# Scan of a delta-rule layer: the state's decay product moved from VectorE to GpSimd

## The chip, the cores and the metric

The kernel runs on one core of a Trainium2 chip. The metric is the device time of one execution in microseconds (us), the median over several runs. Engines are called TensorE (PE in profile rows, PEld for its weight loads), VectorE (DVE), ScalarE (ACT), GpSimd (POOL) and SyncE (SP); each works through its own instruction list in order, and they meet only at semaphores.

## The reference

A block of three parts on x of 4 x 1024 tokens, 256 wide: a mixture-of-experts feed-forward layer, an attention-like recurrent layer, and the feed-forward layer again. Only the recurrent layer is touched. Its core, cut to what matters (8 heads of 32, so 4 x 8 = 32 states of 32 x 32):

```
k = l2norm(silu(x @ Wk));  k_ = -beta * k
gk = interleave(log_f, 0);  a = interleave(k_ * exp(log_f), k_);  b = interleave(k, k)
kk, vv, qq = interleave(0, k), interleave(0, v), interleave(0, q)
def step(S, inp):
    g, a_t, b_t, k_t, v_t, q_t = inp
    bS = einsum('bhk,bhkv->bhv', b_t, S)
    S = exp(g)[..., None] * S + a_t[..., None] * bS[:, :, None, :] + k_t[..., None] * v_t[:, :, None, :]
    o = einsum('bhk,bhkv->bhv', q_t, S)
    return (S, o)
```

## The kernel before

The 1024 tokens of a batch row are done in 4 passes of 256 tokens. In each pass a preparing part forms the projections, the decays and the inverses of small triangular matrices, and then a scan carries the states through the pass. The scan has UN = 16 steps of CT = 16 tokens. A step takes a state S of the 32 chains (128 partitions x 256 numbers, in two halves f = 0, 1 of 128 x 128) to the next one. The four passes come one after the other, each scan starts and ends as a block of its own, and the feed-forward layers lie outside.

In step u, for each half f, the work is:

1. TensorE, line 2387 ("r"): the state against the step's decayed keys and queries, `kq`, after the state S[f] of step u-1 is there.
2. VectorE, line 2461 ("Rt"): adds the values `vi`; line 2464 ("R"): transposes in 32 x 32 blocks.
3. VectorE, line 2466 ("D"): D[f] = S[f] times the decay of the whole step, `eg`. It stands behind the transpose R of its half, so ahead of Rt of the second half.
4. After both halves VectorE does line 2452 ("turn"): the transpose of the end keys `kd` **of step u+1**, behind a wait on `s_kd` for step u+1. In steps 6 to 13 of a pass that has another pass behind it, it then does line 2470, the statistics of one row block for the next pass.
5. TensorE, line 2395 ("u"), ScalarE, line 2432 ("U": the copy out of PSUM), TensorE, line 2404 ("d"), in that order for each half; TensorE does u of both halves ahead of d of both. A filler product (line 2409) closes the step.
6. VectorE, line 2475 ("dS"): transposes the state's increment out of PSUM; line 2478 ("S add"): S[f] = D[f] + dS[f], and releases `s_S[f]`. The order is dS 0, S add 0, dS 1, S add 1.

GpSimd forms the operands of a step in `stage` (lines 2345 to 2360): two products at line 2355 and one at 2356 (`kq`), a copy at 2357 (`vi`) and two products at 2359 (`kd`, whose second releases `s_kd`). There are two buffers of each. The stages of steps 0 and 1 are made before the scan opens. In the scan, stage(u+1) waits for r and Rt of step u-1, and for the turn of step u-1, because it writes over their buffer; nothing else stands ahead of it in GpSimd's list. ScalarE makes copies of other operands (2424, 2425) and of the outputs (2435) beside this.

The semaphore `s_S[f]` has value 1 at the start and is raised once in each step, so "s_S[f] at least u+1" means that step u-1 has stored its state. `s_dec[f]` says that D[f] of a step is done.

Of the kernel before, what the change touches and what calls it, by code (L numbers as in the profile page):

```python
# [10 lines left out]
ALU = mybir.AluOpType  # L11
ACT = mybir.ActivationFunctionType
AX = mybir.AxisListType
P = 128
# [27 lines left out]
HEADS, HD = 8, 32  # L42
# [4 lines left out]
CT = 16  # L47
SUB = 2 * CT
UN = 16
PT = CT * UN  # L50
PASSES = SEQ // PT
GS = CT + 1
# [1857 lines left out]
def invert_and_scan(nc, scope, sb, sem, psum, s, nxt, env, z, a_sb, a_top, tk, s_tk, tm):  # L1910
# [8 lines left out]
    zz, pr = tb("zz", [P, HQ * CT * CT]), tb("pr", [P, 3, HQ * CT * CT])  # L1919
    pr_all = pr[:, :, :].rearrange("p n x -> p (n x)")  # L1920
    steps = scan(sem, psum, s, env, z, nxt, a_sb[:, :, :].rearrange("p g c -> p (g c)")[:, SUB * HQ * SUB:], ng, pr_all, zz)

    s_zero, s_one, s_tp, s_ev, s_fine = sem("zero"), sem("one"), sem("tp"), sem("gev"), sem("fine")
# [373 lines left out]
def scan(sem, psum, s, env, z, nxt, home0, home1, home2, home3):  # L2297


    k, q, kb, v, eg, ek, ta, S, ident = (env[n] for n in "k q kb v eg ek ta S ident".split())  # L2300
    o, xa, stats, s_pre, s_nxt = env["o"], env["xa"], env["stats"], z["pre"], z["nxt"]
    NT = BATCH * PT // P
    HC = CHAINS // 2
# [3 lines left out]
    def carve(home, shapes):  # L2307
# [11 lines left out]
    Rt, R, D, U = halves[0:2], halves[2:4], halves[4:6], halves[6:8]  # L2319
# [9 lines left out]
    s_r, s_u, s_d, s_Rt, s_R, s_dec, s_dS, s_S, s_U, s_O = ([sem(f"{n}{f}") for f in range(2)] for n in  # L2329
        ("r", "u", "d", "Rts", "Rs", "dec", "dSs", "Ss", "Us", "Os"))  # L2330
# [14 lines left out]
    def stage(pool, u, b, first):  # L2345
        def t(x, at=0, step=CT):
            return x[:, :, bass.ds(u * step + at, CT)]
        if not first:
            pool.wait_ge(s_r[1], u - 1)
            pool.wait_ge(s_kr, u - 1)  # L2350
            pool.wait_ge(s_Rt[1], u - 1)
        keys = kq[b][:, :, 0:SUB].rearrange("p c (t r) -> p c t r", r=2)
        ends = kd[b].rearrange("p c (t r) -> p c t r", r=2)
        for r in range(2):
            pool.tensor_tensor(keys[:, :, :, r], t(kb), t(eg, r, GS), ALU.mult)
        pool.tensor_tensor(kq[b][:, :, SUB:KQ], t(q), t(eg, 1, GS), ALU.mult).then_inc(s_kq, 1)
        pool.tensor_copy(vi[b][:, :, :, 1], t(v)).then_inc(s_vi, 1)
        for r in range(2):
            i = pool.tensor_tensor(ends[:, :, :, r], t(k), t(ek, r, GS), ALU.mult)
        i.then_inc(s_kd, 1)  # L2360

    def open_gpsimd(pool, u):
        pool.memset(vi[u][:, :, :, 0:1], 0.0).then_inc(s_pad, 1)
        stage(pool, u, u, True)

    def gpsimd(pool):
        with pool.Fori(1, UN // 2) as j:
            for b in range(2):
                stage(pool, 2 * j + b, b, False)

    def tensor(pe):
        def step(u, b):
# [75 lines left out]
    def vector(dve):  # L2448
        def turn(u, b):
            dve.wait_ge(s_kd, u + 1)  # L2450

            dve.transpose(ar[b][:, :, CT:KQ], kd[b][:, :, :]).then_inc(s_kr, 1)

        def step(u, b, last, row=None):
            for f in range(2):
                ch = slice(HC * f, HC * f + HC)
                if f == 0:
                    dve.wait_ge(s_vi, u + 1)
                dve.wait_ge(s_r[f], u + 1)

                dve.tensor_tensor(Rt[f][:, :, :], vi[b][:, ch, :, :].rearrange("p c t r -> p c (t r)"),
                                  b_p[f][:, :, 0:SUB], ALU.add).then_inc(s_Rt[f], 1)
                dve.wait_ge(s_Rt[f], u + 1)
                dve.transpose(R[f][:, :, :], Rt[f][:, :, :]).then_inc(s_R[f], 1)  # L2464
                dve.wait_ge(s_S[f], u + 1)
                dve.tensor_tensor(D[f][:, :, :], S[:, ch, :], eg[:, ch, bass.ds(u * GS + CT, 1)].to_broadcast([P, HC, HD]), ALU.mult).then_inc(s_dec[f], 1)
            if not last:
                turn(u + 1, 1 - b)
            if row is not None:
                dve.bn_stats(stats[:, bass.ds(row, 1), :].rearrange("p a s -> p (a s)"),  # L2470
                             xa[:, bass.ds(row, 1), :].rearrange("p a d -> p (a d)")).then_inc(s_stat, 1)
            for f in range(2):
                ch = slice(HC * f, HC * f + HC)
                dve.wait_ge(s_d[f], u + 1)
                dve.transpose(dS[f][:, :, :], b_p[f][:, :, KQ:RO]).then_inc(s_dS[f], 1)
                dve.wait_ge(s_dec[f], u + 1)
                dve.wait_ge(s_dS[f], u + 1)
                dve.tensor_tensor(S[:, ch, :], D[f][:, :, :], dS[f][:, :, :], ALU.add).then_inc(s_S[f], 1)
        for f in range(2):
            dve.sem_inc(s_S[f], 1)  # L2480
        dve.wait_ge(s_pad, 2)
        turn(0, 0)
        step(0, 0, False)
        step(1, 1, False)
        with dve.Fori(1, STAT // 2) as j:
            for b in range(2):
                step(2 * j + b, b, False)
        if nxt is not None:
            dve.wait_ge(s_nxt, 16 * BATCH)
        with dve.Fori(STAT // 2, (STAT + NT) // 2) as j:  # L2490
            for b in range(2):
                step(2 * j + b, b, False, 2 * j + b - STAT if nxt is not None else None)
        step(UN - 2, 0, False)
        step(UN - 1, 1, True)
        if nxt is not None:
            dve.wait_ge(s_stat, NT)

    return Scan(sync, open_gpsimd, gpsimd, tensor, open_scalar, scalar, vector)


# [58 lines left out]
```

## Time and profile before

| | |
|---|---|
| median of 3 runs | 1867.22 us (1866.78 to 1869.74) |
| the profiled execution's own time | 1866.42 us |
| its span in the profile | 1864.6 us |
| busy in the span: PE, DVE, ACT, POOL | 1593.2, 1126.5, 774.5, 760.1 us |
| the four scans | 64 steps; the first runs from 641.2 to 708.5 us |
| mean granted TensorE clock | 0.932 of full |

The span is what the profile records; some 2 us lie around it. Timeline rows have the start, the duration, the engine, the line, the operation, the tile written and read, how many instructions are merged in the row, and in brackets how long the engine had been idle and which engine's work ended that.

### The profile page before, as it was taken

How to read it: one execution, taken by the hardware profiler on the slowest of the kernel's cores; microseconds unless marked ns; L12 is line 12 of the kernel's file. 1: busy time of each engine (PE TensorE's matmuls, PEld its weight loads, DVE VectorE, ACT ScalarE, POOL GpSimd, SP SyncE). 2: the span in 40 equal slices, each digit the busy share in tenths (PEclk: the TensorE clock that was granted, in tenths of full speed). 3: DMA queues.
4: the chain of work that ended last, by engine and by line, in shares of the span. 5: the costliest groups of instructions: out<-in, count | busy, mean ns of one | idle time of the engine just before them, and what ended most of it. 6: DMA issues, size and time to landing. Idle time of an engine off the chain costs nothing. (4 is left out here: it accounts for less than half of the span.)

```text
span 1864.6 us, 69187 instructions
## 1 busy us (share of the span) xinstructions
PE 1593.2 (85%) x26524; PEld 1302.6 (70%) x26525; DVE 1126.5 (60%) x3424; ACT 774.5 (42%) x1805; POOL 760.1 (41%) x944
## 2 busy tenths in 40 slices
PE   5499999999577988788888788887885999999994
PEld 5499999999435565355654556545564999999994
DVE  7646434444357786877868778688774546444341
ACT  2143333333267334673346733467332443333331
POOL 2554422222154651646516465164651234422221
PEclk9999999999779898798987999889897999999997
DMA  9563433232300200002000020000102833332334
GB/s 300 184 187 76 88 48 48 45 51 45 74 4 7 70 22 24 4 7 70 22 23 4 7 70 23 23 4 7 47 23 83 255 78 76 75 64 47 49 48 113
DMA packets 84233, 116.23 MB, mean 62 GB/s; under 512 B 12952, under 2 KB 74464, under 8 KB 82016
## 3 DMA queue, kind: packets, MB, share of 16 engines
q1 hardware_dynamic: 56160, 74.17, 13.1%
q0 software_dynamic: 27360, 37.80, 11.5%
q10 hardware_dynamic: 608, 2.96, 0.5%
q8 instruction: 54, 0.88, 0.2%
q14 instruction: 51, 0.42, 0.1%
HBM read 64.87 MB, written 54.21 MB: 64 GB/s over the span
## 5 line engine op out<-in xcount | busy, mean ns | idle before, releaser
L1065 POOL DMA_INDIRECT x<-ffn_yout,ffn_place x142 | 222.6, 1568 | 531.6 <-DVE ffn_yout L997 454.6
L1003 DVE TENSOR_TENSOR ffn_inner<-ffn_inner,ffn_bank 128x512 f32<-128x512 f32 x142 | 97.6, 687 | 349.2 <-PE ffn_bank L873 346.8
L873 PE MATMUL ffn_bank<-ffn_tileT,ffn_gate_now 128*128 128x128 f32 x2272 | 280.2, 277 | 0.0
L873 PE MATMUL ffn_bank<-ffn_tileT,ffn_up_now 128*128 128x128 f32 x2272 | 277.6, 275 | 0.0
L954 ACT ACTIVATE ffn_inner<-ffn_bank 128x512 f32<-128x512 f32 x142 | 84.8, 597 | 459.0 <-PE ffn_bank L873 459.0
L883 PE MATMUL ffn_bank<-ffn_w,ffn_inner 128*128 x1136 | 268.9, 380 | 1.7 <-DVE ffn_yout L997 1.7
L873 PEld LDWEIGHTS ffn_bank<-ffn_tileT,ffn_gate_now 128*128 128x128 f32 x2272 | 268.4, 194 | 0.1
L873 PEld LDWEIGHTS ffn_bank<-ffn_tileT,ffn_up_now 128*128 128x128 f32 x2272 | 266.1, 193 | 0.0
L883 PEld LDWEIGHTS ffn_bank<-ffn_w,ffn_inner 128*128 128x128 f32 x1136 | 205.0, 190 | 24.4 <-issue 2.5
L816 ACT COPY ffn_gate_now<-ffn_w 128x1024 f32 x142 | 148.4, 1045 | 29.9 <-issue 22.3
L816 DVE COPY ffn_up_now<-ffn_w 128x1024 f32 x142 | 99.6, 702 | 55.3 <-issue 43.9
L428 POOL DMA_INDIRECT xs<-at_kept_rows,at_kept_slots x64 | 78.8, 1231 | 115.7 <-ACT pass_aq L2218 73.7
L428 POOL DMA_INDIRECT xs<-ffn_rows,ffn_slot_u x80 | 80.1, 1001 | 51.6 <-DVE ffn_slot_u L335 27.8
L1860 PEld LDWEIGHTS at_bank<-at_ta 32*32 32x32 f32 x4096 | 61.1, 125 | 43.2 <-issue 43.0
L1860 PE MATMUL at_bank<-at_ta 32*32 32x48 f32 x4096 | 66.1, 227 | 13.6 <-DVE at_ta L1733 10.7
L997 DVE TENSOR_SCALAR ffn_yout<-ffn_bank,ffn_weight 128x256 f32<-128x256 f32 x142 | 67.4, 474 | 0.0
L2395 PE MATMUL at_wide<-pass_ng,pass_pr 32*32 32x32 f32 x3072 | 44.4, 196 | 26.1 <-DVE pass_ng L2464 12.6
L1870 PE MATMUL at_bank<-at_tm,at_consts 128*32 128x384 f32 x256 | 36.2, 644 | 29.8 <-POOL at_tm L1777 21.8
L2395 PEld LDWEIGHTS at_wide<-pass_ng,pass_pr 32*32 32x32 f32 x3072 | 36.5, 109 | 35.3 <-issue 35.3
L2404 PE MATMUL at_bank<-pass_pr,pass_ng 32*32 32x48 f32 x3072 | 54.7, 208 | 7.3 <-issue 2.3
L2228 ACT COPY at_ta<-at_bank 128x512 f32<-128x512 f32 x48 | 26.2, 593 | 80.3 <-PE at_bank L2124 79.1
L2432 ACT COPY pass_ng<-at_wide 128x128 f32<-128x128 f32 x96 | 25.5, 265 | 78.6 <-PE at_wide L2395 78.5
(574 smaller groups left out, 3179.3 us busy)
## 6 DMA issues: line engine op xcount, KB each, us to landing
ffn_w<-in_w1t_dram SPq DMA_DIRECT2D x16, 1024.0 KB, 5.6
ffn_tile<-xs SPq DMA_DIRECT2D x122, 130.0 KB, 2.1
ffn_w<-in_w2t_dram SPq DMA_DIRECT2D x16, 512.0 KB, 6.9
at_a_sb<-x SPq DMA_DIRECT2D x32, 256.0 KB, 2.8
ffn_x<-in_x_dram SPq DMA_DIRECT2D x16, 256.0 KB, 5.5
x<-ffn_x SPq DMA_DIRECT2D x16, 256.0 KB, 6.1
x<-at_a_sb SPq DMA_DIRECT2D x16, 256.0 KB, 2.1
xs<-ffn_empty SPq DMA_DIRECT2D x23, 130.0 KB, 2.9
```

The source lines that it names most:

```text
L428: pool.indirect_dma_start(xs, bass.IndirectOffsetOnAxis(ap=slot_u[:, c, i:i + 1], axis=0), rows[:, i, :], None).then_inc(s_scat, 16)
L816: copy(half_now[half][b][:, :, :], src.rearrange("p e k f -> p (e k) f")).then_inc(s_now[half], 1)
L873: t = pe.matmul(bank[:, i * P:(i + 1) * P], half_now[half][b][:, k, i * P:(i + 1) * P], rowsT[b][:, k * P:(k + 1) * P], start=(k == 0), st ...
L883: t = pe.matmul(p_y, inner[b][:, k * P:(k + 1) * P], w2[:, bass.ds(e * 1024 + k * DIM, DIM)], start=(k == 0), stop=(k == ICH - 1))
L954: act.activation(inner[b][:, :], p_g[b][:, :], ACT.Silu).then_inc(s_silu, 1)
L997: dve.tensor_scalar(yout[b][:, :], p_y, weight[b][:, 0:1], None, ALU.mult).then_inc(s_ys, 1)
L1003: dve.tensor_tensor(inner[b][:, :], inner[b][:, :], p_u[b][:, :], ALU.mult).then_inc(s_act, 1)
L1065: pool.indirect_dma_start(total, bass.IndirectOffsetOnAxis(ap=place[b][:, 0:1], axis=0), yout[b][:, :], None, compute_op=ALU.add).then_inc ...
L1860: t = pe.matmul(bank[r, uu * 2 * RW:(uu + 1) * 2 * RW], lo[r, u0 + uu, :, :].rearrange("p l c -> p (l c)"), hi[r, u0 + uu, :, :].rearrange ...
L1870: t = pe.matmul(p_f[x * HD:(x + 1) * HD, 0:UN // 4 * FE], headcol[:, :], prod[b][:, x * UN // 4 * FE:(x + 1) * UN // 4 * FE], start=True, ...
L2395: tiles(lambda c, r: pe.matmul(b_u[f][r, c * HD:(c + 1) * HD], tu[b][r, ch + c, :], R[f][r, c, :], start=True, stop=True)).then_inc(s_u[f], 1)
L2404: tiles(lambda c, r: pe.matmul(b_p[f][r, c, SUB:RO], U[f][r, c, :], ar[b][r, ch + c, :], start=False, stop=(c == HC - 1), skip_group_check ...
```

## The change

The product D is taken out of VectorE's list and put into GpSimd's. There D of step u stands ahead of the stage of step u+1, each half behind a wait for the state that step u-1 stores. It keeps its operands, its output and the semaphore that it raises.

```
     def open_gpsimd(pool, u):
         pool.memset(vi[u][:, :, :, 0:1], 0.0).then_inc(s_pad, 1)
         stage(pool, u, u, True)
 
+    def decayed(pool, u):
+        for f in range(2):
+            ch = slice(HC * f, HC * f + HC)
+            pool.wait_ge(s_S[f], u + 1)
+            pool.tensor_tensor(D[f][:, :, :], S[:, ch, :], eg[:, ch, bass.ds(u * GS + CT, 1)].to_broadcast([P, HC, HD]), ALU.mult).then_inc(s_dec[f], 1)
+
     def gpsimd(pool):
+        decayed(pool, 0)
         with pool.Fori(1, UN // 2) as j:
             for b in range(2):
+                decayed(pool, 2 * j + b - 1)
                 stage(pool, 2 * j + b, b, False)
+        decayed(pool, UN - 1)
```

and in VectorE's step, behind the transpose R of each half:

```
                 dve.transpose(R[f][:, :, :], Rt[f][:, :, :]).then_inc(s_R[f], 1)
-                dve.wait_ge(s_S[f], u + 1)
-                dve.tensor_tensor(D[f][:, :, :], S[:, ch, :], eg[:, ch, bass.ds(u * GS + CT, 1)].to_broadcast([P, HC, HD]), ALU.mult).then_inc(s_dec[f], 1)
```

## Rows read from the trace of the kernel before

**Rows 1.** One step of the first pass, step 10, on VectorE: the timeline
```profile
684.81 0.31 DVE L2464 STREAM_TRANSPOSE pass_ng<-pass_ng 128x128 f32<-128x128 f32 x1
685.05 0.25 DVE L2466 TENSOR_TENSOR pass_ng<-at_S,at_eg 128x128 f32<-128x128 f32 x1
...
685.22 0.28 DVE L2461 TENSOR_TENSOR pass_ng<-at_a_sb,at_bank 128x128 f32<-128x128 f32 x1
...
685.93 0.43 DVE L2452 STREAM_TRANSPOSE pass_pr<-pass_ng 128x256 f32<-128x256 f32 x1
...
686.29 0.38 DVE L2470 BATCH_NORM_STATS2 at_stats<-at_a_sb  x1
...
686.85 0.32 DVE L2475 STREAM_TRANSPOSE pass_zz<-at_bank 128x128 f32<-128x128 f32 x1 [0.17 <-PE at_bank L2404]
...
687.27 0.61 DVE L2478 TENSOR_TENSOR at_S<-pass_ng,pass_zz 128x128 f32<-128x128 f32 x1
```

**Rows 2.** Timeline: GpSimd's stage(11), and step 9's S add of half 1
```profile
681.22 0.28 DVE L2461 TENSOR_TENSOR pass_ng<-pass_ng,at_bank 128x128 f32<-128x128 f32 x1
...
681.85 0.90 POOL L2355 TENSOR_TENSOR pass_ng<-at_qb,at_eg 128x128 f32 x2 [1.59 <-DVE pass_ng L2461]
...
683.36 0.94 POOL L2359 TENSOR_TENSOR pass_ng<-at_kfk,at_ek 128x128 f32 x2
...
683.52 0.32 DVE L2475 STREAM_TRANSPOSE pass_zz<-at_bank 128x128 f32<-128x128 f32 x1
...
683.94 0.51 DVE L2478 TENSOR_TENSOR at_S<-pass_ng,pass_zz 128x128 f32<-128x128 f32 x1
```

**Rows 3.** Timeline: TensorE's r of half 1 in step 10; the last step's end and what follows
```profile
684.59 0.54 PE L2387 MATMUL at_bank<-at_a_sb,at_S 32*32 32x48 f32 x32 [0.24 <-DVE at_S L2478]
...
707.54 0.29 DVE L2478 TENSOR_TENSOR at_S<-pass_ng,pass_zz 128x128 f32<-128x128 f32 x1
...
708.21 0.29 DVE L2478 TENSOR_TENSOR at_S<-pass_ng,pass_zz 128x128 f32<-128x128 f32 x1
709.57 1.28 ACT L1424 ACT_TABLE_LOAD   x1 [1.22 <-PEq L70]
```

**Rows 4.** Timeline: the Rt add that opens steps 2, 6 and 14
```profile
651.90 0.29 DVE L2461 TENSOR_TENSOR pass_ng<-at_a_sb,at_bank 128x128 f32<-128x128 f32 x1 [0.89 <-PE at_bank L2387]
...
668.21 0.29 DVE L2461 TENSOR_TENSOR pass_ng<-at_a_sb,at_bank 128x128 f32<-128x128 f32 x1
...
700.76 0.29 DVE L2461 TENSOR_TENSOR pass_ng<-at_a_sb,at_bank 128x128 f32<-128x128 f32 x1
```

**Rows 5.** One line's instructions: durations in ns, minimum/median/maximum, of D and one stage product
```profile
L2466 DVE TENSOR_TENSOR pass_ng<-at_S,at_eg x96: 247/249/251, 641.8 to 1172.4; 128x128 f32<-128x128 f32 x96
...
L2356 POOL TENSOR_TENSOR pass_ng<-at_qb,at_eg x24: 411/433/456, 638.1 to 1165.3; 128x128 f32 x21, 128x128 f32<-128x128 f32 x3
```

**Rows 6.** Timeline: a wait of GpSimd outside the loop, and its shortest stage
```profile
636.82 0.28 DVE L2071 TENSOR_TENSOR pass_a_top<-pass_a_top,pass_pr 128x128 f32<-128x128 f32 x1
...
637.15 0.21 POOL L2363 MEMSET pass_ng<- 128x128 f32 x1 [1.94 <-DVE pass_a_top L2071]
...
690.01 0.82 POOL L2355 TENSOR_TENSOR pass_ng<-at_qb,at_eg 128x128 f32 x2 [1.86 <-DVE pass_ng L2461]
...
691.40 0.83 POOL L2359 TENSOR_TENSOR pass_ng<-at_kfk,at_ek 128x128 f32 x2
```

**Rows 7.** Timeline: step 1, where TensorE is late
```profile
645.38 0.29 DVE L2478 TENSOR_TENSOR at_S<-pass_ng,pass_zz 128x128 f32<-128x128 f32 x1
...
649.66 0.32 DVE L2475 STREAM_TRANSPOSE pass_zz<-at_bank 128x128 f32<-128x128 f32 x1 [1.96 <-PE at_bank L2404]
```

**Rows 8.** Stretches: busy us (count) of PE, PEld, DVE, ACT, POOL; granted clock; DMA share; GB/s
```profile
644.00:648.00 4.00, 2.11 (x105) 1.56 (x91) 3.22 (x11) 0.93 (x4) 1.71 (x5) 1.00 0.45 152
648.00:652.00 4.00, 3.77 (x179) 3.35 (x183) 1.24 (x5) 1.46 (x6) 1.56 (x5) 0.65 0.02 4
656.00:704.00 48.00, 38.90 (x2296) 31.88 (x2296) 40.19 (x139) 17.30 (x71) 26.13 (x66) 1.00 0.07 22
```

## The prediction

> **What bounds the kernel now.** I read the busy table first: TensorE 85% of the span, GpSimd 41%. That is an average over stages, and it says nothing about a scan, so I went to the timeline of one step. Inside a scan TensorE is busy 38.90 us of 48 and GpSimd 26.13 us of 48 [rows 8]: both have gaps, and a step is a chain through several engines. It takes 4.08 us where VectorE has no statistics (16.31 us for the four steps from 651.90 to 668.21) and 4.07 us where it mostly has (32.55 us for the eight to 700.76) [rows 4]. The statistics cost next to nothing, because VectorE still waits 0.17 us for TensorE's d behind them [rows 1]. The scan's last S add ends at 708.50 and the next block opens behind it [rows 3], so what the 64 steps gain or lose goes whole into the time.
>
> Two things in the step matter here. First, the slot of D: the transpose R starts at 684.81, D at 685.05, Rt of the second half at 685.22 [rows 1]. Second, GpSimd's slack. Stage(11) runs from 681.85 to 684.30 [rows 2], and VectorE's turn, which waits for its last product, comes at 685.93 [rows 1]: it is 1.63 us early. It is early only because it may start 0.35 us behind Rt of step 9 (681.50), while step 9 still has its second half to go [rows 2].
>
> **What is removed.** Two D of 249 ns on VectorE in each step [rows 5]. D of half 0 holds Rt of half 1 back by at most its slot, 0.17 us. But Rt of half 1 also needs TensorE's r of half 1, which began at 684.59, 0.63 us before it [rows 3]. The r's own last product ends at 685.13, so at most 0.1 of the 0.17 us is free in a step like this; D of half 1 stands ahead of the turn, in time that VectorE spends waiting. I take 0.15 us for a step that isn't held otherwise, and nothing where GpSimd holds it.
>
> **What is moved, and past what.** D(u) now stands ahead of stage(u+1) in GpSimd's list, and its second half waits for S add 1 of step u-1. The stage behind it has no need of that state, but it queues behind the wait. The turn of step u waits for that stage, and in VectorE's list dS and both S adds of step u stand behind the turn. So a new ring closes: S add 1 of step u-1, D, the stage, turn, dS, S add, dS, S add 1 of step u. Its length, from the end of one S add 1 to the end of the next:
>
> - GpSimd wakes: the nearest rows are 0.35 us in the loop, with three waits and computed addresses [rows 2], and 0.05 us outside it (637.10 to 637.15) [rows 6]. D has one wait and an address to compute: 0.25 us.
> - D on GpSimd: same size as a product of the stage, 433 ns (411 to 456) [rows 5]: 0.43. That is 1.7 times VectorE's 249 ns.
> - The stage: 2.45 us (681.85 to 684.30) [rows 2], or 2.22 (690.01 to 692.23) [rows 6]: 2.35.
> - VectorE wakes for the turn: no row has VectorE waiting for GpSimd. TensorE began 0.14 us after the S add that freed it (684.45 to 684.59) [rows 2, 3], the shortest wait of GpSimd was 0.05, the longest 0.35: I take 0.10.
> - Turn to the next instruction: 0.36 us (685.93 to 686.29). With statistics 0.38 more, no longer hidden [rows 1].
> - dS 0 to S add 0: 0.42 (686.85 to 687.27) [rows 1].
> - S add 0's start to S add 1's end: 0.96 undisturbed (707.54 to 708.50) [rows 3]. Here GpSimd's D 0 of the next step begins some 0.54 us in (0.29 and the 0.25 of the wake) and ends at 0.97; S add 1 would begin at 0.67. An S add under a GpSimd product ends 0.15 us behind it (684.30 and 684.45) [rows 2]. So 0.97 and 0.15, some 1.14, of which 0.18 is contention.
>
> The sum is 0.25+0.43+2.35+0.10+0.36+0.42+1.14 = 5.05 us, and 5.43 with statistics: 0.97 and 1.36 us more than now. TensorE's path doesn't come close. In step 10 dS 0 followed the end of step 9's S add 1 by 2.40 us (684.45 to 686.85) [rows 1, 2], and in the ring it follows by 3.49.
>
> **How many steps.** Step 0 has its stage beforehand, and step 15 has no stage behind its D: both keep the old chain and gain 0.15. Step 1 is already late by TensorE: its dS 0 begins 3.99 us after the S add 1 before it ended (645.67 to 649.66) [rows 7], later than the ring's 3.49, so only the 0.18 is added. That leaves 13 steps: in the first three passes 8 with and 5 without statistics, 8 x 1.36 + 5 x 0.97 + 0.18 - 0.30 = 15.6 us; in the last 13 x 0.97 + 0.18 - 0.30 = 12.5 us. In all 3 x 15.6 + 12.5 = 59.3 us. On the profiled execution's own 1866.4 that gives 1925.7; the median of the runs is 0.8 above it, so 1927.
>
> **The port.** An S add, with two inputs in SBUF, was stretched from 0.29 to 0.51 and 0.61 us, while a dS transpose out of PSUM kept its 0.32 under a running stage product [rows 1 to 3]. No row has an Rt add (one input in SBUF, one in PSUM) under a GpSimd product; in the changed kernel all of them are. If they took turns, each would hold the stage back by up to its 0.28 us, 0.56 a step, and the ring would be 5.6 us.
> The Trainium skill, SBUF — State Buffer, Who interferes with whom, says that a VectorE instruction with at most one SBUF input doesn't contend with GpSimd. By that rule the Rt adds cost nothing and the sum stays; without it 52 steps pay up to 0.56 us each, 29 us.
>
> **Rivals.**
> 1. *The Rt adds (or GpSimd's added waits) lengthen the ring*, by about half of the 0.56: 0.3 us in 52 steps is 16 us, 1943. For it: the S adds show that the two engines do block each other. Against: the dS row. 12%.
> 2. *TensorE's clock.* After a stretch in which TensorE was busy 2.11 of 4 us, the granted clock of the next was 0.65 [rows 8]. In the ring it would be busy some 3.3 of 5.1 to 5.4 us, so it may fall to 1.2 GHz. In the ring this is mostly hidden: with every product chain longer by half, d's result comes at about 3.6 instead of 2.4 us after S add 1, against the turn's end at 3.5. Steps 0, 1 and 15 would pay about 0.9 us each: 4 x 3 x 0.9 = 11 us, 1938. 13%.
> The Trainium skill, TensorE: Matmul & The Clock Gate, What's actually happening, has it that the slow level is the default and activity releases it; that speaks for this rival, as does the 0.65.
> 3. *Faster: GpSimd takes D in its idle time*, and only VectorE's slot is left to count: up to 64 x 0.17 = 11 us, less what r of half 1 takes back, so 1860. For it: GpSimd idles 1.59 us ahead of a stage [rows 2]. It decides by one place: stage(11) must end before the turn's old slot, 685.93, thus 1.48 us after the S add at 684.45, where wake, D, stage and wake need 3.13. Against it stands the order of the list: the idle time lies ahead of the old stage, and the new wait uses all of it. 3%.
> 4. *Only contention*: the ring has cover that I don't see and the S adds alone are stretched: 0.18 x 56 is 10 us, less 64 x 0.05 to 0.10: about 1872. 2%.
>
> **How the numbers follow.** The ring as summed has 69%; 1% is left for no change. The unknown costs at their low ends (wake 0.05, D 0.41, stage 2.22, turn's wake 0.05, no contention) take 0.58 us off 52 steps, 30 us; at their high ends (0.36, 0.46, 2.46, 0.35, the full 0.61 of an S add) they add 0.64, 33 us. They will hardly all fall on one side: two thirds of that is 1907 and 1949, and the upper side takes in rivals 1 and 2, so 1907 to 1952. About 0.2% is what a measurement of this kernel can tell from no change. Faster by over 0.2%: 0.03; within: 0.01; slower: 0.96.
>
> **What would show it.** The Rt adds that open steps 2 to 14 stand 5.0 to 5.5 us apart, wider by 0.3 to 0.4 where there are statistics. VectorE's longest idle time in a step lies ahead of line 2452 (the turn), released by GpSimd's second `kd` product. GpSimd's D 1 begins 0.05 to 0.36 us behind S add 1 and its stage runs on without a gap. S add 1 takes 0.4 to 0.6 us, S add 0 takes 0.29. The idle time ahead of dS, put down to TensorE, is gone. Steps 0 and 15 keep some 4 us. If the turn doesn't wait and steps stay near 4.0, the ring is wrong and rival 3 holds; if the Rt adds or the stage's products are longer than before, it is rival 1; if the granted clock within the scans is well under 1, rival 2.

## The result, and the profile after

The changed kernel takes 1904.83 us (median of 4 runs, 1903.83 to 1906.46) against 1868.48 us for the kernel before beside it: a ratio of 1.0196, 95% interval 1.0179 to 1.0212. It is slower by 36 us. Forecast were 59 us, with a range from 1907 to 1952, so the direction held and the size didn't: the time lies 2 us under the range.

A step of the scan in the timeline (step 10 of the first pass, from the S add that ends step 9; VectorE's and GpSimd's rows, where [rows 1, 2] have those of before):

```profile
679.07 0.44 DVE L2485 TENSOR_TENSOR at_S<-pass_ng,pass_zz 128x128 f32<-128x128 f32 x1
...
679.60 0.29 DVE L2470 TENSOR_TENSOR pass_ng<-pass_ng,at_bank 128x128 f32<-128x128 f32 x1
...
679.70 0.41 POOL L2370 TENSOR_TENSOR pass_ng<-at_S,at_eg 128x128 f32<-128x128 f32 x1 [0.33 <-DVE at_S L2485]
...
680.06 0.83 POOL L2355 TENSOR_TENSOR at_a_sb<-at_qb,at_eg 128x128 f32 x2
680.26 0.29 DVE L2470 TENSOR_TENSOR pass_ng<-pass_ng,at_bank 128x128 f32<-128x128 f32 x1
...
681.46 0.83 POOL L2359 TENSOR_TENSOR at_a_sb<-at_kfk,at_ek 128x128 f32 x2
...
682.32 0.45 DVE L2461 STREAM_TRANSPOSE pass_pr<-at_a_sb 128x256 f32<-128x256 f32 x1 [1.43 <-POOL at_a_sb L2359]
...
682.69 0.38 DVE L2477 BATCH_NORM_STATS2 at_stats<-at_a_sb  x1
683.00 0.29 DVE L2482 STREAM_TRANSPOSE pass_zz<-at_bank 128x128 f32<-128x128 f32 x1
...
683.39 0.29 DVE L2485 TENSOR_TENSOR at_S<-pass_ng,pass_zz 128x128 f32<-128x128 f32 x1
...
683.87 0.41 POOL L2370 TENSOR_TENSOR pass_ng<-at_S,at_eg 128x128 f32<-128x128 f32 x1 [1.58 <-DVE at_S L2485]
...
684.02 0.40 DVE L2485 TENSOR_TENSOR at_S<-pass_ng,pass_zz 128x128 f32<-128x128 f32 x1
```

Lines have moved: D is L2370, Rt L2470, the turn L2461, dS L2482, the S add L2485. The ring can be read off row by row. S add 1 ends at 679.51, GpSimd's D 1 starts at 679.70, the stage at 680.06 and without a gap to 682.29; VectorE has stood idle for 1.43 us and starts the turn at 682.32; then come the statistics, dS, S add 0, dS, S add 1, which ends at 684.42. dS has no idle time in front of it: TensorE's result has long been there. In [rows 1] the turn had none and dS had 0.17 us.

The instructions of the turn's line in the whole run (first their durations in ns, then what the idle time ahead of them waited for, in us and times):

```profile
L2461 DVE STREAM_TRANSPOSE pass_pr<-at_a_sb x24: 402/445/447, 644.1 to 1199.0; 128x256 f32<-128x256 f32 x24
...
  POOL at_a_sb L2359: 35.7, 26
  POOL pass_ng L2359: 28.2, 21
  POOL end_ng L2359: 9.6, 7
```

54 turns waited for GpSimd's `kd` product, 73.5 us in all; there were none before. The scans grew by less than half of that (below), since much of it stands in the place of other idle time: VectorE idled 34.6 us ahead of dS before and 16.5 after.

The steps, taken from the timelines of both kernels as the distance from one S add 1's end to the next, in us, first pass, steps 1 to 15:

```
before  5.34 4.90 4.09 4.13 4.04 4.05 4.09 4.10 4.04 4.05 4.08 4.10 4.04 3.78 4.00
after   5.42 4.75 4.59 4.55 4.68 5.07 4.91 4.88 4.99 5.08 4.90 4.88 4.97 4.61 4.04
```

Over all passes, with steps 3 to 14 as the body of a scan: the 24 with statistics went from a mean of 4.08 to 4.96, the 24 without from 4.03 to 4.63. That is 24 x 0.887 + 24 x 0.596 = 35.6 us. Steps 0, 1, 2 and 15 gave back 2.4 us in all. The four scans took 275.7 us before (from the first Rt add to the last S add) and 308.9 after: 33.2 us more. The span grew by 40.0 us (1864.6 to 1904.6) in the profiled executions. The remaining 6.8 us lie outside the scans; 4.9 of them lie ahead of the first Rt add (641.2 before, 646.2 after), where the eight other kernels measured beside a kernel before of some 1868 us, six of them with a D on GpSimd ahead of it too, have 640.4 to 643.2. In these eight profiled executions and the kernel before's own the part outside the scans took from 1588.9 to 1593.5 us, and in that of the changed kernel 1595.7, so I count it as scatter of that execution. Of the 36 us between the medians some 3 are left that no step shows.

### The profile page after: what moved, and what is told of

Its sections match the earlier page's. It is cut to its first block and busy times, and to the rows that moved or that the text cites. A ratio compares the mean times of both kernels' runs of the same rounds, so it can differ in the third digit from the quotient of the medians.

```text
span 1904.6 us, 69207 instructions
## 1 busy us (share of the span) xinstructions
PE 1623.4 (85%) x26524; PEld 1328.7 (70%) x26525; DVE 1102.5 (58%) x3296; ACT 775.9 (41%) x1805; POOL 803.9 (42%) x1072
## 5 line engine op out<-in xcount | busy, mean ns | idle before, releaser
L2370 POOL TENSOR_TENSOR pass_ng<-at_S,at_eg 128x128 f32<-128x128 f32 x96 | 39.0, 408 | 96.2 <-DVE at_S L2485 96.2
L2444 ACT COPY at_tm<-at_bank 128x64 f32 (+1 forms) x128 | 27.2, 213 | 105.2 <-DVE pass_zz L2482 79.7
L2404 PE MATMUL at_wide<-pass_ng,pass_pr 32*32 32x32 f32 x3072 | 48.8, 206 | 20.6 <-issue 8.5
L2413 PE MATMUL at_bank<-pass_pr,pass_ng 32*32 32x48 f32 x3072 | 59.6, 227 | 4.9 <-issue 1.7
L2404 PEld LDWEIGHTS at_wide<-pass_ng,pass_pr 32*32 32x32 f32 x3072 | 40.6, 119 | 30.1 <-issue 29.5
```

The costliest lines, as they stand in the source:

```text
L2370: pool.tensor_tensor(D[f][:, :, :], S[:, ch, :], eg[:, ch, bass.ds(u * GS + CT, 1)].to_broadcast([P, HC, HD]), ALU.mult).then_inc(s_dec[f], 1)
L2404: tiles(lambda c, r: pe.matmul(b_u[f][r, c * HD:(c + 1) * HD], tu[b][r, ch + c, :], R[f][r, c, :], start=True, stop=True)).then_inc(s_u[f], 1)
L2413: tiles(lambda c, r: pe.matmul(b_p[f][r, c, SUB:RO], U[f][r, c, :], ar[b][r, ch + c, :], start=False, stop=(c == HC - 1), skip_group_check ...
```

## The experiments

The table gives each kernel's time against the kernel before measured beside it, and, from one profiled execution each, its steps 3 to 14 (us, mean of 24 and 24; before: 4.08 and 4.03, scans 275.7).

```
                               ratio (95%)               steps with / without statistics   scans
changed kernel                 1.0196 (1.0179 to 1.0212)   4.96   4.63                     308.9
stage ahead of D               1.0000 (0.9990 to 1.0009)   4.11   4.07                     275.4
before + the wait only         1.0136 (1.0119 to 1.0152)   4.73   4.49                     301.7
D on VectorE behind both R     0.9984 (0.9975 to 0.9994)   4.11   3.98                     271.8
changed, turn behind S adds    0.9968 (0.9956 to 0.9979)   3.94   3.98                     268.3
changed, kd products first     0.9947 (0.9932 to 0.9963)   3.87   3.85                     265.0
changed, D of half 0 only      1.0024 (1.0013 to 1.0035)   4.36   4.10                     281.0
changed, D of half 1 only      1.0214 (1.0191 to 1.0237)   4.95   4.82                     316.0
changed, wide filler           1.0190 (1.0168 to 1.0212)   4.96   4.61                     310.3
changed, copy vi last          1.0114 (1.0097 to 1.0130)   4.74   4.38                     298.5
before, kd products first      0.9996 (0.9986 to 1.0006)   4.01   4.03                     272.7
kd first, D of half 0 only     0.9953 (0.9937 to 0.9968)   3.87   3.90                     266.0
```

### Is it the order of GpSimd's list?

```
                 for b in range(2):
-                decayed(pool, 2 * j + b - 1)
                 stage(pool, 2 * j + b, b, False)
+                decayed(pool, 2 * j + b - 1)
```

> The changed kernel with the two lines in GpSimd's loop exchanged: the stage of step u+1 first, the two D of step u behind it. Theory (the cost is the order of GpSimd's list: the wait for the state stands ahead of the stage): no turn waits any more, the steps are back at 4.0 to 4.1 us, and with VectorE's slot of 0.17 us free they may be up to 0.1 shorter; time between 8 us below and 3 us above the kernel before. Rival (GpSimd's two products themselves, or their contention with VectorE, make the cost): the steps stay at 4.6 to 5.0 us and the time some 30 us above the kernel before.

1868.4 us against 1868.9: the whole loss is gone with two lines exchanged. The same products on the same engine, with the same wait, cost nothing when the stage that the turn waits for stands ahead of them. The gain hoped for doesn't come either, and the timeline shows why (a step of the first pass):

```profile
680.74 0.56 DVE L2485 TENSOR_TENSOR at_S<-pass_ng,pass_zz 128x128 f32<-128x128 f32 x1
680.75 0.88 POOL L2359 TENSOR_TENSOR at_a_sb<-at_kfk,at_ek 128x128 f32 x2
...
681.59 0.40 POOL L2370 TENSOR_TENSOR pass_ng<-at_S,at_eg 128x128 f32<-128x128 f32 x1
681.64 0.51 DVE L2485 TENSOR_TENSOR at_S<-pass_ng,pass_zz 128x128 f32<-128x128 f32 x1
```

The S adds, two SBUF inputs each, are under a GpSimd product and take 0.56 and 0.51 us for 0.29. In the kernel before one of the two was stretched in 44 of the 48 steps 3 to 14 and never both; here both are in 32. On the mean of the steps with statistics dS 0 comes 0.09 us earlier behind S add 1 than before (2.39 us for 2.48), and from there to the next S add 1's end it takes 0.12 us longer (1.72 for 1.60).

### The wait without the products

```
             for b in range(2):
+                pool.wait_ge(s_S[1], 2 * j + b)
                 stage(pool, 2 * j + b, b, False)
```

> The kernel before, with D left on VectorE, and only a wait for S add 1 of the step before put ahead of each stage on GpSimd. Theory (ring through the wait): from S add 1's end wake 0.2 to 0.3, stage 2.3, turn 0.03 and 0.37, dS 0.40, S adds 0.92: some 4.2 us, and 4.5 to 4.6 with statistics, so 0.15 and 0.5 us a step more than before, 13 to 19 us in all; half of the change's cost without any product moved. Rival (the moved products are the cost): no change against the kernel before, within 3 us.

1893.2 us, 24 us above the kernel before. The wait alone makes two thirds of the change's cost. It is more than the 13 to 19 us expected. D is still on VectorE, and GpSimd's stage now lies under it:

```profile
684.92 0.29 DVE L2479 TENSOR_TENSOR at_S<-pass_ng,pass_zz 128x128 f32<-128x128 f32 x1
...
685.59 0.84 POOL L2355 TENSOR_TENSOR at_a_sb<-at_qb,at_eg 128x128 f32 x2 [2.39 <-DVE at_S L2479]
...
686.01 0.56 DVE L2467 TENSOR_TENSOR pass_ng<-at_S,at_eg 128x128 f32<-128x128 f32 x1
...
686.39 0.51 POOL L2356 TENSOR_TENSOR at_a_sb<-at_qb,at_eg 128x128 f32 x1
...
688.03 0.45 DVE L2453 STREAM_TRANSPOSE pass_pr<-at_a_sb 128x256 f32<-128x256 f32 x1 [0.74 <-POOL at_a_sb L2359]
```

D takes 0.56 us instead of 0.25, but VectorE has the time: it still idles 0.74 us ahead of the turn. What counts is the other side. The third stage product takes 0.51 us here for 0.42 in the changed kernel, and the whole stage 2.40 us on the mean of 48 steps, where 2.3 was expected and the changed kernel has 2.26. The stage starts 0.21 or 0.37 us behind the S add's end (here 685.21 to 685.59), 0.29 on the mean. The rest of the excess wasn't taken apart.

### What VectorE's slot is worth

Both D stay on VectorE and move behind the second transpose R.

```
                 dve.transpose(R[f][:, :, :], Rt[f][:, :, :]).then_inc(s_R[f], 1)
+            for f in range(2):
+                ch = slice(HC * f, HC * f + HC)
                 dve.wait_ge(s_S[f], u + 1)
                 dve.tensor_tensor(D[f][:, :, :], S[:, ch, :], ...
```

> The kernel before with both D still on VectorE, but behind the second transpose R and not between the transposes: what the slot itself is worth. Theory: Rt of half 1 is bound by TensorE's r of half 1 in most steps and by the slot in few: 0.05 to 0.15 us a step, so 3 to 9 us faster. Rival (D between the transposes costs nothing): within 2 us.

1865.9 against 1868.9: 2.9 us less, at the lower edge of what was expected. Without statistics the steps are 0.05 us shorter; with them they gain nothing (4.11 for 4.08), since two D, the turn and the statistics in a row now end behind TensorE's result.

### The turn out of the way

```
             if not last:
-                turn(u + 1, 1 - b)
...
                 dve.tensor_tensor(S[:, ch, :], D[f][:, :, :], dS[f][:, :, :], ALU.add).then_inc(s_S[f], 1)
+            if not last:
+                turn(u + 1, 1 - b)
```

> The changed kernel, GpSimd's order as it is, with the turn of step u+1 moved on VectorE from ahead of dS to behind both S adds. Theory (the cost reaches the chain through the turn alone): dS waits for TensorE again, and the turn, 0.37 us, now lies ahead of Rt of the next step but partly beside r: steps of 4.0 to 4.3 us, time 0 to 15 us above the kernel before. Rival (GpSimd's load or its port is the bound): steps stay above 4.6 us, 30 us above.

1863.2 us: faster than the kernel before, where at best no change was expected. GpSimd's list is that of the changed kernel, with D ahead of the stage. So the late stage does harm only through the turn. What was missed in the expectation is that the turn lies almost wholly beside TensorE's r (against the kernel before, the first Rt add comes 0.16 us later behind S add 1 and the second no later, 0.81 us for 0.85), and that the S adds are no longer under the stage. S add 0 takes 0.29 us (S add 1 still some 0.41, under D 0 of the next step), and dS waits for TensorE again:

```profile
682.56 0.85 POOL L2359 TENSOR_TENSOR at_a_sb<-at_kfk,at_ek 128x128 f32 x2
...
683.02 0.32 DVE L2480 STREAM_TRANSPOSE pass_zz<-at_bank 128x128 f32<-128x128 f32 x1 [0.73 <-PE at_bank L2413]
683.44 0.29 DVE L2483 TENSOR_TENSOR at_S<-pass_ng,pass_zz 128x128 f32<-128x128 f32 x1
```

### Only what stands between the state and `kd`

First the change with the two `kd` products put at the head of the stage:

```
+        for r in range(2):
+            i = pool.tensor_tensor(ends[:, :, :, r], t(k), t(ek, r, GS), ALU.mult)
+        i.then_inc(s_kd, 1)
         for r in range(2):
             pool.tensor_tensor(keys[:, :, :, r], t(kb), t(eg, r, GS), ALU.mult)
         pool.tensor_tensor(kq[b][:, :, SUB:KQ], t(q), t(eg, 1, GS), ALU.mult).then_inc(s_kq, 1)
         pool.tensor_copy(vi[b][:, :, :, 1], t(v)).then_inc(s_vi, 1)
-        for r in range(2):
-            i = pool.tensor_tensor(ends[:, :, :, r], t(k), t(ek, r, GS), ALU.mult)
-        i.then_inc(s_kd, 1)
```

> The changed kernel with the wait, the D products and VectorE's list as they are; only inside GpSimd's stage the two end-key products (kd) come first and the products for kq and the copy vi behind them. Theory (the turn waits for the last product of the stage): kd is now ready some 0.18+0.36+0.85 = 1.4 us behind S add 1 instead of 2.8, the turn has its old place without a wait, and the rest of the stage still ends ahead of the next r. Steps of 3.75 to 3.95 us, time 5 to 15 us below the kernel before. Rival (GpSimd's load as such, 3.1 us of products a step, or the port is the bound): steps stay above 4.5 us, 30 us above the kernel before.

1858.5 us against 1868.6: 10 us faster than the kernel before. Nothing but the order within the stage differs from a kernel that is 36 us slower. (Here L2355 is `kd`, L2358 and L2359 are `kq`.)

```profile
683.95 0.40 POOL L2370 TENSOR_TENSOR pass_ng<-at_S,at_eg 128x128 f32<-128x128 f32 x1 [0.33 <-DVE at_S L2485]
...
684.31 0.88 POOL L2355 TENSOR_TENSOR pass_ng<-at_kfk,at_ek 128x128 f32 x2
...
685.22 0.45 DVE L2461 STREAM_TRANSPOSE pass_pr<-pass_ng 128x256 f32<-128x256 f32 x1
...
686.18 0.32 DVE L2482 STREAM_TRANSPOSE pass_zz<-at_bank 128x128 f32<-128x128 f32 x1 [0.20 <-PE at_bank L2413]
```

The turn comes at 685.22, just behind the products' end at 685.19, with no idle time marked. It is still `kd` that releases it, but that no longer matters: dS waits for TensorE. Then one product's share: the change with the copy `vi` alone moved behind `kd`.

```
-        pool.tensor_copy(vi[b][:, :, :, 1], t(v)).then_inc(s_vi, 1)
         for r in range(2):
             i = pool.tensor_tensor(ends[:, :, :, r], t(k), t(ek, r, GS), ALU.mult)
         i.then_inc(s_kd, 1)
+        pool.tensor_copy(vi[b][:, :, :, 1], t(v)).then_inc(s_vi, 1)
```

> The changed kernel with GpSimd's copy vi moved behind the two kd products; the wait, the D products and the total work stay. Theory (what counts is what stands between the state and the last kd product): the copy's 0.25 us leaves the ring, so steps of 4.35 and 4.6 to 4.8 us and 52 x 0.25 = 13 us less than the changed kernel, 23 above the kernel before. Rival (GpSimd's load counts, wherever it stands): within 3 us of the changed kernel.

1900.2 us, with the kernel before at 1877.8 beside it: 22 us above it, as expected, where the change is 36 above. The steps are 0.23 and 0.25 us shorter, the copy's own slot of 0.25. So this product, standing ahead of `kd` in the ring, counts in full.

Third, the control: the edit of the first diff of this section (`kd` first) in the kernel before.

> A control: the kernel before, D on VectorE, with only the stage's order changed (kd first). Theory: the turn never waited there, so the order gives nothing: within 3 us of the kernel before, and what the kernel with both edits gained (10 us) is the gain of D's move. Rival (the gain was the order's own): 8 to 10 us faster than the kernel before.

1877.4 against 1877.8, interval -0.14% to +0.06%: no change. At most 2.6 us of the 10 could be the order's own (in the profiled executions the scans are 3.0 us shorter); the rest needs D's move.

### Which half

GpSimd makes D of one half only; VectorE's D of the other half stays where it was in the kernel before. For half 0:

```
     def decayed(pool, u):
-        for f in range(2):
+        for f in (0,):
...
                 dve.transpose(R[f][:, :, :], Rt[f][:, :, :]).then_inc(s_R[f], 1)
+                if f == 1:
+                    dve.wait_ge(s_S[f], u + 1)
+                    dve.tensor_tensor(D[f][:, :, :], S[:, ch, :], ...
```

> The changed kernel with only D of half 0 on GpSimd; D of half 1 is back on VectorE behind its transpose. GpSimd's wait is then for S add 0, which ends some 0.7 us ahead of S add 1. Theory (ring from the state waited for, through stage and turn): 0.18+0.37+2.3+0.03+0.37+0.40+0.29 = 3.95 us, 4.25 with statistics, so the product chain of 3.9 to 4.05 binds without statistics and the ring only with them: 0 to 8 us above the kernel before. Rival (each product on GpSimd costs its own share): half of the change's cost, 18 us above.

1873.0 against 1868.6 us: 4 above. The wait is for S add 0, 0.7 us earlier, and most of the ring's length beyond the product chain goes with it. The steps, 4.10 and 4.36, are 0.11 to 0.15 longer than summed; 0.07 of that is the stage, which VectorE's D 1 again lies over (2.37 us for the 2.3 taken).

And for half 1 (`for f in (1,)` on GpSimd, `if f == 0` on VectorE):

> The changed kernel with only D of half 1 on GpSimd; D of half 0 is back on VectorE between the transposes. GpSimd's wait is for S add 1 as in the changed kernel. Theory: the ring is the same but for S add 1, which no product on GpSimd stretches now (0.29 for 0.41 us): 4.5 us, 4.85 with statistics, 4 to 8 us below the changed kernel, 29 to 33 above the kernel before. Rival (each product costs its own share): 18 us above the kernel before, as with half 0.

1910.3 against 1868.6 us: 42 above, where the change with both halves moved is 36 above; the two intervals overlap. That refutes a share for each product, since this one alone costs no less than both. It also shows that a stretched S add isn't needed for the loss: both S adds take 0.29 us here. But my own figure, some 30, was missed as well. The fourth pass shows what I had left out:

```profile
1391.43 0.29 DVE L2470 TENSOR_TENSOR end_ng<-end_ng,at_bank 128x128 f32<-128x128 f32 x1 [0.89 <-PE at_bank L2396]
...
1391.98 0.48 DVE L2476 TENSOR_TENSOR end_ng<-at_S,at_eg 128x128 f32<-128x128 f32 x1
...
1393.44 0.45 DVE L2461 STREAM_TRANSPOSE end_pr<-at_a_sb 128x256 f32<-128x256 f32 x1 [0.43 <-POOL at_a_sb L2359]
...
1394.51 0.32 DVE L2485 STREAM_TRANSPOSE end_zz<-at_bank 128x128 f32<-128x128 f32 x1 [0.62 <-PE at_bank L2413]
```

and the stretch around it (busy us and counts, then the granted clock):

```profile
1386.00:1402.00 16.00, 14.50 (x605) 12.68 (x597) 9.22 (x30) 4.42 (x18) 8.20 (x22) 0.50 0.07 17
```

TensorE is granted half its clock (1.2 GHz) here, and its chain, with VectorE's D 0 back in it and stretched to 0.48 us under a stage product, is longer than the ring: dS waits 0.62 us for TensorE behind the turn. Such steps take 5.3 to 5.4 us. Where the clock is full, the steps of the same pass take 4.45 to 4.70, near the 4.5 expected.

Last, both edits together, D of half 0 alone on GpSimd and `kd` first:

> Kd first, and D of half 0 alone on GpSimd; D of half 1 on VectorE, behind its transpose where VectorE waits anyway. Theory: the slot between the transposes is what D's move frees, and it is D of half 0's: the same gain as with both halves moved, steps of 3.85 to 3.95 us, within 3 us of that kernel (1858). Rival (D of half 1 holds the turn and dS back too): 3 to 6 us slower than it.

A ratio of 0.9953 beside 0.9947 for both halves: the same. It is D of half 0 that sits in the chain; D of half 1 lies where VectorE waits.

### TensorE's clock

```
-            spin(128)
+            spin(512)
```

> The changed kernel with the filler product at the end of a step four times as wide (512 columns for 128), so that TensorE is busy in the time in which VectorE waits for the turn. Theory (TensorE's clock, which falls in the changed kernel's scans, is hidden in the ring): the granted clock in the scans goes up to 1.0, the steps stay at 4.6 and 4.9 to 5.1 us, time within 3 us of the changed kernel. Rival (the lower clock is part of the cost): steps shorter where the clock was low, 6 to 11 us below the changed kernel.

1901.4 us, and the changed kernel 1904.8: ratios of 1.0190 and 1.0196, whose intervals cover each other. A stretch of the second pass, first with the wide filler, then in the changed kernel:

```profile
896.00:960.00 64.00, 52.74 (x2619) 36.51 (x2620) 38.82 (x128) 19.41 (x79) 37.12 (x98) 0.99 0.05 16
```

```profile
896.00:960.00 64.00, 50.29 (x2540) 42.18 (x2534) 38.36 (x124) 19.24 (x79) 38.34 (x101) 0.81 0.06 17
```

The clock went from 0.81 to 0.99 and the steps stayed: 4.96 with statistics in both, 4.61 and 4.63 without. Over steps 3 to 15 of the four passes the granted clock was 0.86 to 0.97 in the changed kernel and 1.00 with the wide filler. In the changed kernel the lower clock is hidden by the ring.

## Why the prediction was right and wrong

**Right: what happens.** The forecast named the ring, its parts and its place. The turn is where VectorE waits, released by the second `kd` product; S add 1 is stretched (0.39 to 0.45 us in 54 of the 64 steps) and S add 0 isn't (0.29); steps with statistics are longer by 0.3 to 0.4; the fourth pass, which has none, has no step beyond 4.83 us from step 3 on. Exchanging the two lines takes away all of the cost, moving the turn or `kd` does too, and one copy's slot comes back one for one.

**Wrong: the length of the ring.** It was summed as 5.05 and 5.43 us; it is 4.63 and 4.96, so the steps forecast as 5.0 to 5.5 us apart stand 4.55 to 5.08 apart. This is the step of the prediction that failed: the ring was the right one, and nearly every term of its sum was too large. In the step shown above, with statistics, each term against its value in the sum:

```
                            summed  measured
GpSimd wakes                 0.25    0.19   679.51 to 679.70
D on GpSimd                  0.43    0.36   679.70 to 680.06
the stage                    2.35    2.23   680.06 to 682.29 (others up to 2.36)
VectorE wakes                0.10    0.03   682.29 to 682.32
turn to statistics           0.36    0.37   682.32 to 682.69
statistics to dS             0.38    0.31   682.69 to 683.00
dS 0 to S add 0              0.42    0.39   683.00 to 683.39
S add 0 to S add 1's end     1.14    1.03   683.39 to 684.42
sum                          5.43    4.91
```

Every term but one is smaller. D, dS and the statistics were entered with their durations, or from a row with a wait ahead of it (dS in [rows 1]: 0.32 us long, here 0.29); back to back they take less, because an instruction starts 0.05 to 0.08 us before the one ahead of it has ended (D: 0.41 us long, 0.36 to the next). That is 0.17 of the 0.52 us. The two wakes are 0.13 and the stage 0.12. The last term, 0.11, isn't contention sized wrongly: S add 1 ends 0.14 us behind D 0 (684.28 to 684.42), as [rows 2] had it, but D 0 itself comes early, since the same wake was taken too long a second time; and 0.97 and 0.15 are 1.12, not 1.14. The second mistake is in the range, which rested on "they will hardly all fall on one side". Nearly all did: an error of habit, such as rounding each unknown up, isn't independent from term to term. The bound with all low ends, 30 us below, was 1897 and would have held the time. 0.47 us in 24 steps and 0.37 in 24 are 20 us of the 26 by which the scans' part was overrated (59.3 forecast, 33.2 measured); the steps without statistics lose 0.37 and not 0.42 because they took 4.03 us before, not 4.08.

**Wrong: step 2.** It was counted as an ordinary step of the ring, 0.97 us longer. In the kernel before it already took 4.89 to 5.29 us, and after 4.75 to 5.12. That is 4 x 0.97 plus the 0.5 us it gave back, 4.4 of the 26. The rows on step 1 showed TensorE late; the step behind it wasn't looked at. Steps 0, 1 and 15 together gave back 2.0 us where 0.5 was forecast. (The 0.15 us for the freed slot stood against the prediction's own bound of 0.1; D behind both R, which frees it for both halves, gave 2.9 us in 64 steps.)

**The rivals.** Rival 1 falls: 55 of the 64 Rt adds of half 1 lie under a stage product and none takes more than 0.29 us, and the products are no longer than before (0.83 for two; the stage 2.26 us on the mean for 2.37). The Trainium skill, SBUF — State Buffer, Who interferes with whom, says just that of an instruction with one SBUF input, and the trace agrees. Rival 2 came half true: the clock does fall, to 0.81 in the stretch above against 1.00 in [rows 8], but the wide filler shows that it costs nothing within the resolution. It does cost with D of half 0 in TensorE's chain (half 1 alone on GpSimd). Rival 3 fell for the changed kernel, since the order of the list decides; with `kd` first GpSimd does take D in its idle time, and the 1860 us were nearly met (1858.5), though the gain isn't the slot alone (last point below). Rival 4 comes nearest to the kernel with the stage ahead of D: the 0.12 us of contention and the 0.09 gained ahead of dS nearly cancel.

## What to carry to other kernels

Moving an instruction to an idle engine moves its wait too, and on an engine that works in order everything behind that wait becomes as late as what it waits for (here the wait without the product cost 24 of the 36 us); look for whoever waits for the last thing in the queue, and follow the ring back to its start. The remedy was the order of the products behind the wait: the one that the other engine needs first comes first, and a change of +2.0% became one of -0.5%. When summing a ring, take start-to-start distances of back-to-back instructions, and let a range reach to where all unknown terms err the same way.

## What was not expected of the hardware

- In the changed kernel GpSimd's product under a wait started 0.18 to 0.22 us behind the S add that released it, and 0.08 outside the loop, where the nearest rows had 0.35 and 0.05; VectorE started 0.03 us behind GpSimd's last product.
- D took 0.41 us on GpSimd (406 to 417 ns in all 128 cases), 1.6 times VectorE's 0.25. But D on VectorE under GpSimd's products took up to 0.57 us, and made the stage longer as well (2.40 us for 2.26 in the kernel with the wait only).
- At a granted clock of 0.50 a scan step with D 0 on VectorE and D 1 on GpSimd took 5.3 to 5.4 us for 4.45 to 4.70 at full clock: TensorE's chain became longer than the ring.
- The gain of the best version has two parts. From S add 1's end to dS 0 its steps 3 to 14 are 0.07 us shorter than before on the mean (the freed slot lies there), and from dS 0 to the next S add 1's end, where the S adds no longer lie under the stage (0.29 and mostly 0.36 to 0.44 us), 0.13 shorter with statistics and 0.10 without. No run changes one of the two alone in this kernel.
